# Alternating the gate products of the first two blocks, with the banks of slots and projection swapped once

## The reference

```python
# layer 0
y  = einsum('bct,bcd->bdt', x, cond_w[idx7])       # 64x64 mixing matrix of each sample
gu = einsum('bsd,hd->bsh', y, ternary_quant(w_gate_up)); gate, up = split(gu)
h  = silu(gate) * up                               # 2048 hidden columns
hn = h * rsqrt(mean(h*h) + eps)
x1 = x + einsum('bsh,dh->bsd', hn, ternary_quant(w_proj))
# layer 1
hh = x1 @ W.T + ((x1 @ A[idx6].T) @ B[idx6].T) * s # linear product with adapters
logits = (hh @ router_w.T + router_b)              # 8 experts for each output column
c   = top-2 of softmax(logits), renormalised
out = x1 + sum_e c[e] * (hh @ expert_w[e].T + expert_b[e])
```

## Time and profile before

| | |
|---|---|
| time, median of 3 runs | 2211.55 us (2211.19 to 2212.24) |
| the profiled execution | 2213.71 us, span 2212.0 us |
| PE busy | 2193.9 us, 99% of the span |
| DVE busy | 1625.1 us, 73% |
| ACT busy | 1053.5 us, 48% |
| mean granted clock of TensorE | 0.998 of full speed |

### The profile page before, as it was taken

One profiled execution on the slowest core, in us unless ns is written; L12 is line 12 of the kernel. 1 busy time (PEld: TensorE's weight loads), 2 busy tenths in 40 slices (PEclk: granted clock), 3 DMA queues, 4 the chain that ended last, 5 costly groups with the idle time before them and its releaser, 6 DMA issues.

```text
span 2212.0 us, 28768 instructions
## 1 busy us (share of the span) xinstructions
PE 2193.9 (99%) x9817; PEld 1810.9 (82%) x9817; DVE 1625.1 (73%) x2119; ACT 1053.5 (48%) x1493; POOL 63.8 (3%) x83
## 2 busy tenths in 40 slices
PE   7999999999999999999999999999999999999999
PEld 5778888888888888888888888888888888888887
DVE  8986444444444445689999999999898888888883
ACT  6764333333333233588777878777332222222221
POOL 0000000101111102000000000000000000000000
PEclk9999999999999999999999999999999999999999
DMA  6313303232424224412212121116222222222220
GB/s 210 105 53 126 98 20 105 83 107 81 111 80 109 92 58 143 157 67 81 81 71 85 71 85 71 63 68 262 103 100 85 81 85 81 95 71 100 66 85 24
DMA packets 157908, 205.66 MB, mean 93 GB/s; under 512 B 63330, under 2 KB 96674, under 8 KB 155682
## 3 DMA queue, kind: packets, MB, share of 16 engines
q1 hardware_dynamic: 114578, 149.95, 20.5%
q10 hardware_dynamic: 43152, 55.06, 7.6%
q0 software_dynamic: 128, 0.07, 0.0%
HBM read 136.35 MB, written 68.68 MB: 93 GB/s over the span
## 4 chain that ended last, share of the span: by engine, by line
PE 94%; issue 4%; DVE 1%; POOL 1%; ACT 0%; DMA 0%; POOLq 0%; DVEq 0%; ACTq 0%
PE slot L1657 19%; PE ex_bank L1834 10%; PE ex_bank L1833 10%; PE ex_bank L1832 10%; PE pj L1670 9%; PE high_bank L1799 5%; PE high_bank L1803 5%; PE high_bank L1801 5%; PE low_bank L1799 4%; PE low_bank L1803 4%; PE low_bank L1801 4%; PE slot L1719 3%; PE slot L1626 1%; PE slot L1708 1%; PE ex_bank L1847 1%
## 5 line engine op out<-in xcount | busy, mean ns | idle before, releaser
L1657 PE MATMUL slot<-y_hi,wgu 128*128 128x512 f32 x1024 | 402.5, 393 | 1.2 <-ACT wgu L768 0.6
L1657 PE MATMUL slot<-y_lo,wgu 128*128 128x512 f32 x1024 | 399.3, 390 | 0.0
L1832 PE MATMUL ex_bank<-ew_hi,hb 128*128 128x512 f32 x992 | 385.9, 389 | 0.0
L1833 PE MATMUL ex_bank<-ew_hi,hb 128*128 128x512 f32 x992 | 385.9, 389 | 0.0
L1834 PE MATMUL ex_bank<-ew_lo,hb 128*128 128x512 f32 x992 | 385.9, 389 | 0.0
L1104 ACT ACTIVATE ex_bank<-eb_sb 128x512 f32<-128x512 f32 x248 | 149.3, 602 | 451.1 <-DVE acc L1563 391.5
L1513 DVE SCALAR_TENSOR_TENSOR lead_in<-code_in,wts 128x1024 bf16<-128x1024 bf16 x256 | 311.7, 1218 | 7.5 <-ACT wts L1044 5.8
L1657 PEld LDWEIGHTS slot<-y_hi,wgu 128*128 128x128 f32 x1024 | 192.8, 188 | 44.8 <-DVE q_scale L1174 2.9
L1657 PEld LDWEIGHTS slot<-y_lo,wgu 128*128 128x128 f32 x1024 | 192.7, 188 | 39.8
L1216 DVE TENSOR_TENSOR hid<-gate,slot 128x512 f32<-128x512 f32 x112 | 76.9, 687 | 192.0 <-ACT gate L784 191.3
L1832 PEld LDWEIGHTS ex_bank<-ew_hi,hb 128*128 128x128 f32 x992 | 186.2, 188 | 38.7
(11 more groups left out here) (169 smaller groups left out, 3500.8 us busy)
## 6 DMA issues: line engine op xcount, KB each, us to landing
hb<-h_scratch SPq DMA_DIRECT2D x34, 512.0 KB, 3.3
code_scratch<-half_code SPq DMA_DIRECT2D x32, 512.0 KB, 2.6
half_in<-code_scratch SPq DMA_DIRECT2D x32, 512.0 KB, 3.3
hb<-h_scratch ACTq DMA_DIRECT2D x30, 512.0 KB, 3.6
h_scratch<-ht ACTq DMA_DIRECT2D x48, 256.0 KB, 3.0
q_raw<-in_w_ffn SPq DMA_DIRECT2D x21, 512.0 KB, 3.4
x_scratch<-x_res ACTq DMA_DIRECT2D x8, 1024.0 KB, 4.5
lead_scratch<-lead SPq DMA_DIRECT2D x32, 256.0 KB, 2.0
```

The lines of the kernel that those rows point to most:

```text
L1657: last = mm(slot[s % 2][:, g, :], wgu[:, c, r * P:(r + 1) * P], y[:, c, :], start=(c == 0 and v == 0), stop=(c == DC - 1 and v == 1))
L1832: mm(ex[e][:, :], hb[:, u, c, 0, :], ew_hi[:, e, c, :], start=False, stop=False, skip_group_check=True)
L1833: mm(ex[e][:, :], hb[:, u, c, 1, :], ew_hi[:, e, c, :], start=False, stop=False, skip_group_check=True)
```

## The change

In the first two blocks, `gu(1, j)` now stands right behind `gu(0, j)`, from pair 0 on. For that block 1's mixing (`second_mix`) stands right behind block 0's, and it writes to the banks of the sums instead of slots. Half of its gathers of mixing matrices go from SP's queue to POOL's. Slots and sums of the first part lie in each other's banks (`slot_first`, `pj_first`), so that block 1's sums don't wait until block 0's are read. `quant_mean` copies the scales of two units in three. DVE's `finish` is split in `variance` and `residual`, and the squares of block 1 are separated from its low parts. `gu(1, 14)` and `gu(1, 15)` no longer stand between `squares(0)` and `proj(1, 0)`. Transposes, `adapt` and `linear` stand two or three projections later, `small_weights` in pair 6, `linear_weights` behind p = 6. The work of every engine is the same but for the scales. The order of SP's queue quoted above is not changed. The core of the diff:

```diff
-GU_ORDER = []
+GU_ORDER = [(i, j) for j in range(HC) for i in range(2)]
...
 def second_ring(p):
-    return 1 if p == HC - 1 else p % 4
+    return (p + 2) % 4
 def second_freed(p):
-    if p < 2:
-        return HC - 1 + p
-    return HC + (HC - 2 if p == HC - 1 else p - 3)
+    return HC - 3 + p
...
+        pfirst = ExitStack()
+        slot_first = [pb(f"slot_first{s}", [P, 2, BLK], pfirst) for s in range(2)]
+        pj_first = pb("pj_first", [P, SUB, D], pfirst)
+        pfirst.close()
+        pj = pb("pj", [P, SUB, D], pa)
         slot = [pb(f"slot{s}", [P, 2, BLK], pa) for s in range(2)]
-        pj = [pb(f"pj{s}", [P, D], pa) for s in range(SUB)]
...
             sp.dma_start(x_res[:, :, :], one(XB, 1)).then_inc(xmix1_in, 16)
-            gather_mix(1, mixw1, mixw1_in, range(3))
+            gather_mix(1, mixw1, mixw1_in, range(SPB // 2))
             load_raw(3)
             load_raw(4)
-            gather_mix(1, mixw1, mixw1_in, range(3, SPB))
...
+            pool.wait_ge(dconst, 2)
+            for q in range(SPB // 2, SPB):
+                v = pool.value_load(subject_i[0:1, SPB + q:SPB + q + 1], min_val=0, max_val=E - 1)
+                r = (q % 2) * C
+                pool.dma_start(mixw1[r:r + C, q // 2, r:r + C], cond_w[bass.ds(v * C, C), :]).then_inc(mixw1b_in, 16)
```

On ACT:

```diff
+            def second_mix():
+                for u in range(2):
+                    act.wait_ge(mix1_filled, u + 1)
+                    nc.scalar.activation(y1_hi[:, 2 * u:2 * u + 2, :], pj_first[:, 2 * u:2 * u + 2, :], ACT.Copy)\
                         .then_inc(act_half, 1)
...
             quant_in(2)
+            second_mix()
             quant_in(3)
...
                 silu(0, j)
                 quant_out(3 * h + 1)
-                if h:
-                    silu(1, j - 2)
                 quant_out(3 * h + 2)
                 act.wait_ge(drained, use(0, f"gu{j}")[0] + 1)
                 square(0, j, hid[:, j % 2, :])
+                silu(1, j)
                 if more:
+                    quant_mean(3 * h + 3)
                     quant_mean(3 * h + 4)
...
-                if h:
-                    silu(1, j - 1)
-                else:
-                    mix(1)
+                silu(1, j + 1)
                 if h < PAIRS - 2:
                     quant_in(3 * h + 6)
-            second_hidden(0)
-            silu(1, HC - 2)
-            for p in range(1, 4):
-                second_hidden(p)
-            silu(1, HC - 1)
+                if h == PAIRS - 2:
+                    small_weights()
+            for p in range(3):
+                second_high(p)
+            second_square(0)
+            second_high(3)
+            second_square(1)
+            second_high(4)
+            second_square(2)
             store_x1(0)
-            small_weights()
-            linear_weights()
+            second_high(5)
+            second_square(3)
             for p in range(4, HC):
-                second_hidden(p)
+                if p >= 6:
+                    second_high(p)
+                second_square(p)
+                if p == 6:
+                    linear_weights()
+                if p in (7, 8):
+                    turn(0, p - 7)
+                if p == 11:
                     adapt(0)
```

On DVE:

```diff
+            def second_mix():
+                for u in range(2):
+                    dve.wait_ge(act_half, act_halves(1, u) + 1)
+                    nc.vector.tensor_tensor(y1_lo[:, 2 * u:2 * u + 2, :], pj_first[:, 2 * u:2 * u + 2, :],
+                                            y1_hi[:, 2 * u:2 * u + 2, :].bitcast(F32), ALU.subtract).then_inc(mix1_drained, 1)
...
             mix(0)
+            second_mix()
...
                     squares(0, j - 1)
-                    second_product(j - 2)
+                second_product(j)
                 if more:
-                    quant_scale(a)
+                    quant_floor(a)
                     quant_gap(a)
...
             squares(0, HC - 1)
+            second_low(0)
+            variance(0)
+            second_low(1)
+            second_low(2)
+            residual(0)
+            squares(1, 0)
+            second_low(3)
+            squares(1, 1)
+            second_low(4)
+            squares(1, 2)
+            second_low(5)
+            squares(1, 3)
             for p in range(4, HC):
+                if p >= 6:
+                    second_low(p)
+                squares(1, p)
+                if p == 6:
+                    linear_weights()
+                if p in (7, 8):
+                    turn(0, p - 7)
```

On PE:

```diff
             mix(0)
+            second_mix()
             quant(2)
             for h in range(PAIRS):
                 j = 2 * h
                 more = h < PAIRS - 1
                 gu(0, j)
-                if h:
-                    gu(1, j - 2)
+                gu(1, j)
...
             squares(0)
-            for j in range(HC - AHEAD, HC):
-                gu(1, j)
             for p in range(HC - 1):
                 proj(1, p, SECOND_ORDER[p])
-                if p in (1, 2):
-                    turn(0, p - 1)
-                if p == 5:
+                if p in (3, 4):
+                    turn(0, p - 3)
+                if p == 8:
                     adapt(0)
-                if p == 7:
+                if p == 10:
                     linear(0, 0)
-                if p == 10:
+                if p == 13:
                     linear(0, 1)
```

More of the change, by code:

```diff
@@ L429, in build, with bank @@
         DFC = diff_dram.rearrange("e p (c o) -> c e p o", c=DC)
+        def bank(n, s):
+            return (slot_first if isinstance(n, int) and n < len(FIRST) else slot)[s % 2]
         def split_slot(i, j):
@@ L1215, in product @@
                 g = gu_count(i, j) % 2 if isinstance(i, int) else j % 2
-                nc.vector.tensor_tensor(hid[:, j % 2, :], gate[:, g, :], slot[s % 2][:, 1, :], ALU.mult).then_inc(drained, 1)
+                nc.vector.tensor_tensor(hid[:, j % 2, :], gate[:, g, :], bank(n, s)[:, 1, :], ALU.mult).then_inc(drained, 1)
             def second_product(j):
@@ L1268, in finish, with residual @@
                     dve.wait_ge(inv_ready, i)
-                nc.vector.tensor_scalar(var[:, :], slot[s % 2][:, 0, 0:SUB], 1.0 / HID, EPS, ALU.mult, ALU.add).then_inc(drained, 1)
+                nc.vector.tensor_scalar(var[:, :], bank(n, s)[:, 0, 0:SUB], 1.0 / HID, EPS, ALU.mult, ALU.add).then_inc(drained, 1)
+            def residual(i):
+                sums = pj_first if isinstance(i, int) and i == 0 else pj
                 dve.wait_ge(inv_ready, i + 1)
@@ L1625, in mix, with second_mix @@
                         for k in range(SUB):
-                            last = mm(slot[s % 2][:, b, k * P:(k + 1) * P], data[:, k, c * P:(c + 1) * P], w[:, k, :],
+                            last = mm(bank(n, s)[:, b, k * P:(k + 1) * P], x_mix[:, k, c * P:(c + 1) * P], mixw[:, k, :],
                                       start=True, stop=True)
                     last.then_inc(filled, 1)
+            def second_mix():
+                pe.wait_ge(xmix1_in, 16)
+                pe.wait_ge(mixw1_in, 8 * SPB)
+                pe.wait_ge(mixw1b_in, 8 * SPB)
+                for c in range(DC):
+                    for k in range(SUB):
+                        last = mm(pj_first[:, c, k * P:(k + 1) * P], x_res[:, k, c * P:(c + 1) * P], mixw1[:, k, :],
+                                  start=True, stop=True)
+                    if c % 2:
+                        last.then_inc(mix1_filled, 1)
             def quant(k):
@@ L1665, in proj @@
                     pe.wait_ge(w_done, UNITS.index(("down", j // 2)) + 1)
-                if j == 0 and not first_block(i):
+                second = isinstance(i, int) and i == 1
+                if j == 0 and first_block(i):
+                    pe.wait_ge(mix1_drained, 2)
+                elif j == 0 and second:
+                    pe.wait_ge(drained, use(1, f"gu{HC - 1}")[0] + 1)
+                elif j == 0:
                     pe.wait_ge(x1_ready, i * SUB)
-                for k in range(SUB):
+                sums = pj_first if first_block(i) else pj
+                for k in reversed(range(SUB)):
+                    if j == 0 and second and k == 0:
+                        pe.wait_ge(drained, use(1, "ss")[0] + 1)
                     for v, h in enumerate(split_slot(i, j)):
-                        last = mm(pj[k][:, :], h[:, k * P:(k + 1) * P], wpj[:, w, :],
+                        last = mm(sums[:, k, :], h[:, k * P:(k + 1) * P], wpj[:, w, :],
                                   start=(j == 0 and v == 0), stop=(j == HC - 1 and v == 1))
@@ L1678, in squares @@
                 for k in range(SUB):
-                    last = mm(slot[s % 2][:, 0, k:k + 1], sumsq[:, k * P:(k + 1) * P], ones_col[:, :], start=True, stop=True)
+                    last = mm(bank(n, s)[:, 0, k:k + 1], sumsq[:, k * P:(k + 1) * P], ones_col[:, :], start=True, stop=True)
                 last.then_inc(filled, 1)
@@ L1707, in adapt @@
```

(2 more changed lines are left out.)

164 lines of the change are left out of this document (68 added, 96 removed).

## The result

The changed kernel takes 2219.13 us (median of 7 runs, 2216.24 to 2220.3), the kernel before 2211.19 beside it (7 runs, 2210.34 to 2212.49). The ratio is 1.0034, its 95% interval 1.0022 to 1.0045: slower by a third of a per cent, 7.9 us. The forecast was 2217.6 in a range of 2212.5 to 2221.0. The profiled execution is the fastest of the seven: 2216.24 us, span 2214.5. The one shown of before was 2.5 us above its median. The two profiles alone therefore show only 2.5 of the 7.9 us.

What follows compares the result with a forecast made beforehand. PE, busy 99% of the span, bounds the kernel, so only waits and clock count: `gu(2, 0)` 2.8 us later plus clock falls of 1.6 and 1.7 make 6.1 us on 2211.55, so 2217.6 us; range 2212.5 to 2221.0.

Steps and rivals of the forecast that it cites:

- Behind block 0: From `squares(0)` to `gu(2, 0)`: 8.8 us of new PE waits, two old ones of 1.8 in all gone.
- S: The end of `squares(0)`, 177.9 us before the change, forecast at 181.2 after it.
- The wait at p = 7: Behind block 0, PE waits 2.5 us for low part 7, which DVE makes only after its split of W.
- The 0.5 at p = 8: Behind block 0, PE waits 0.5 us at p = 8, where a transposed split is ahead.
- The wait at p = 10: Behind block 0, PE waits 5.6 us because `fetch_hid(5)` stands behind `w_lo_ready`, x and eight gathers on SP's queue.
- The start: Up to `gu(0, 2)`: gain 4.2 us from earlier `second_mix`, 2.6 left after a clock fall; bounds 4.2 and 0.8.
- The 1.6 us: Price of a clock fall at `gu(0, 1)`, after PE idles some 2.9 us between 29.2 and 32.6 us.
- POOL's gathers: At the start, half the gathers on POOL's queue cost 0; rival that they come late, 1.8 us more, chance 0.05.
- The pairs: PE leads each pair with 0.4 us slack, cost 0; rival that DVE and ACT lead, 3 us more, chance 0.11.
- The sum: `gu(2, 0)` 2.8 us later, with two clock falls of 1.6 and 1.7 in all 6.1 us: 2217.6 us, chance 0.50.
- one of 1.7 us behind p = 10: The clock falls after PE's 5.6 us idle at p = 10, costing 1.7 us; bounds 0 and 3.4.
- the forecast without the clock: Rival that the clock stays full at the start and behind block 0: 2.8 us slower, 2214.3 us, chance 0.22.

Runs made afterwards that it cites:

- the filled version: Changed kernel with 20 more matmuls on PE between p = 9 and p = 10, output unchanged: 2215.93 us, ratio to the kernel before 1.0021.
- The fetches first: Changed kernel with all ten fetches on SP's queue ahead of the next block's x and gathers: 2211.26 us, ratio to the kernel before 1.0001.
- moving the split alone: Changed kernel with only `linear_weights` moved, from behind p = 6 to behind p = 9 on ACT and DVE: 2223.84 us, ratio 1.0061.
- the repaired version: Changed kernel with all ten fetches first, `linear_weights` behind p = 10 and `small_weights` in pair 7: 2206.54 us, on another chip 2207.43.
- The second traces of both kernels: Both kernels run again with no edit: the changed kernel 2219.66 us (ratio 1.0040), the kernel before 2211.77 us (ratio 1.0002).
- the version with both repairs: Changed kernel with all ten fetches first and `linear_weights` behind p = 10, PE waiting for `w_lo_ready` ahead of `linear(0, 0)`: 2208.55 us, ratio to before 0.9988.

## Why the prediction came out right

*Behind block 0* it holds point by point. From S, forecast and measured: residual over at 4.1 and 4.5 (181.19 + 2.73 less 179.46), split of W done at 16.3 and 16.6, fetch 5 issued at 27.1 and 27.2, p = 10 at 31.4 and 31.35, `gu(2, 0)` without the clock at 60.9 and, in the filled version, 61.0. The wait at p = 7 was 2.5 and is 2.4. The 0.5 at p = 8 is 0 to 0.2. The wait at p = 10 was 5.6; it is 5.2 in one trace and 4.1 in the other, where the slow clock behind p = 7 had already eaten part of it. The fetches first took away the wait at p = 10 and left the one at p = 7; moving the split alone took away the one at p = 7 and, as expected, made the other longer; both together give S+52.6.

*The start* gained more than the sum says. I had `gu(0, 2)` at 42.05; it is at 39.99. The reason is one term that I had left as it was: `mix(0)`. In before it starts at 12.48 and takes 5.45 us at half clock; after it starts at 11.76 and takes 3.82 at full clock, so it ends 2.35 us earlier, and unit 2's `q_scale` (21.74 for 24.1), q4 (29.52 for 32.0) and `gu(0, 1)` (30.18 for 32.6) are all earlier by 2.4 to 2.5. Within that, the two waits of 0.4 and 1.6 us are what was forecast as 2.9. The prediction had overlooked the slow clock under `mix(0)` in the trace of before. Why it is up there in each trace after and down in both before was not isolated, so this part of the gain isn't shown to be the change's. Nor did the clock fall behind the idle time at 30 us in the two traces of the changed kernel; it did in four of the nine of its variants (the fetches first: 0.62 from 30.4 to 33.8). The 1.6 us is right as a price and was wrong as a fixed term of the sum.

*POOL's gathers* cost nothing, as taken. What the Trainium skill (SBUF — State Buffer, section SBUF: two separate sides) says of waiting holds for operations of DVE in a two-port mode. The timeline above shows the gathers 1.14 us apart beside bf16 operations with two inputs and a scale read from PSUM, so no delay is seen at this place; no view shows the mode of these operations, so it is open whether this is a place for that rule, as the prediction has it, and the rule is not tested here. The prediction did not say what they are worth: 4 to 5 us, against the same eight on SP.

*The pairs* cost nothing, as forecast, but the slack of 0.4 us was wrong: the scale on DVE costs its full 0.49 us in each pair. With the alternating order ACT's copy is therefore worth 3 us; what it is worth in the old order was not run. `small_weights` in pair 6 cost 0.6, not 0.2.

*The sum.* For the profiled execution I had `gu(2, 0)` at 242.1 + 1.6 + 1.7 = 245.4, and it is at 241.68. The 3.7 us are 1.7 from S (179.46 for 181.2), 1.6 from the fall at the start that didn't come, and 0.4 from the one behind p = 10. The median nevertheless came out 1.5 us above the forecast. From the 2.5 us of the two profiled executions to the 7.9 of the medians it is 5.4 us: the profiled one of before lies 2.5 above its median, that of the changed kernel 2.9 below. Of the first part 1.6 us is the fall that the other trace of before doesn't have, so gains counted against the earlier trace rows were partly not there. Of the second, 1.9 us is what the slow clock costs by the filled version (3.2) beyond the 1.3 of that profile. The other 1.9 us were not found.

The medians split as 4.7 us (2215.93 less 2211.24, the filled version against before) and 3.2 (the clock, by the fill), for forecast 2.8 and 3.3. That 3.2 and 3.3 agree is luck: the forecast meant one fall at the start and one of 1.7 us behind p = 10, and the fill changes only the second place. The second traces of both kernels, taken together, put `gu(2, 0)` 5.4 us later (243.09 less 237.69), 2.3 of it the clock behind p = 10 and 3.1 the rest, near the 2.8 of the forecast without the clock. The direction and the mechanism behind block 0 are shown; that the total is so near is in part because a start that gained more, and a fall there that didn't come, cancel with a base that was too slow and a dearer clock behind p = 10.

*The change's own aim* does work. With the two waits repaired and `small_weights` moved it is 4 us faster than before; the changed kernel gives that away, and 8 us more, mostly to the order of SP's queue and the place of one split. The 4 us are near the 4.2 forecast for the start, but not the same thing: the forecast was counted against the trace with the fall, and the repaired version also loses the waits of 1.1 and 0.7 us behind block 0.

## What to carry to other kernels

When work is taken out from between two waits, list every queue that this work covered: here two gate products and half a linear product had hidden a DMA queue in which the transfer needed first stood behind eight that nobody waited for. Put transfers in the order of their first use, and a long split behind the last short one that PE waits for. Look at more than one execution before a base is taken: here a fall of the clock was in one and not in the next, and it was two thirds of the excess of the traced execution over its median.

## What the runs showed of the hardware

The same idle time of PE does not always bring the clock down. Ahead of 20 us the kernel before was busy 1.12 of 3.20 us in one execution and 1.05 in another, with 0.50 behind the first and 1.00 behind the second; behind 2.4 us of waiting at p = 7 it was 0.56 in one trace of the changed kernel and 1.00 in the other and in the filled version's. Nor is a fall always equally long: behind p = 10 six matmuls ran slow in one trace and eleven in the other (1.3 and 2.3 us). The Trainium skill (TensorE: Matmul & The Clock Gate, section What's actually happening) says that the count of slow matmuls at a kernel's start differs between runs of one kernel; these traces agree, and show it in the middle of a kernel too. Whether such waits make the times of a kernel spread more is not shown: it is 4.1 us over 7 runs for the changed kernel and 2.8 over 11 with the wait filled, but 3.4 over 11 for the version with both repairs.
